# Copying finished attention contexts out of PSUM on VectorE instead of ScalarE

## The reference

```python
x = x + 0.5 * ffn(layernorm(x))
x = x + attention(layernorm(x))      # 16 heads of 16, causal, softmax, projection w_o and bias b_o
x = x + 0.5 * ffn(layernorm(x))      # the same FFN weights, which are +1 or -1

q, k, v = (h @ w.T split into 16 heads)
scores = q k^T / 4;  masked above the diagonal;  attn = softmax(scores)
ctx = attn @ v                        # (b, h, s, 16)
```

## Time and profile before

| | |
|---|---|
| median of 3 executions | 1556.35 us (1553.98 to 1558.93) |
| the profiled execution | 1555.03 us |
| its span, first to last instruction | 1553.3 us |
| granted clock of TensorE | 1.0 |
| busy: PE, DVE, ACT, POOL | 1533.4, 1118.7, 842.4, 194.9 us |
| chain that ended last | PE 97% |

### The profile page before, as it was taken

The page is one execution under the profiler, slowest core; times in us unless marked ns, Lnnn a source line. Parts: engine busy times, 40 slices in busy tenths (PEclk is TensorE's granted clock), DMA queues, the critical chain, the costliest instruction groups (busy, mean ns, idle before and its releaser), DMA issues.

```text
span 1553.3 us, 35454 instructions
## 1 busy us (share of the span) xinstructions
PE 1533.4 (99%) x14112; PEld 723.7 (47%) x14112; DVE 1118.7 (72%) x1618; ACT 842.4 (54%) x1706; POOL 194.9 (13%) x516
## 2 busy tenths in 40 slices
PE   7999999999999999999999999999999999999999
PEld 3555555555443333334333334333333555555554
DVE  6535543554669999999989998989896667666552
ACT  3223322332168888888888888888886222222221
POOL 4300000000011112121112212212220000000000
DMA  5122023502040222211222221222220222211210
GB/s 161 40 68 58 10 68 95 108 14 68 2 116 23 63 70 62 70 43 46 60 70 63 83 56 53 67 83 65 69 73 25 82 69 71 75 49 61 81 27 14
DMA packets 146275, 96.39 MB, mean 62 GB/s; under 512 B 106592, under 2 KB 125664, under 8 KB 146144
## 3 DMA queue, kind: packets, MB, share of 16 engines
q1 hardware_dynamic: 145712, 94.54, 21.3%
q10 hardware_dynamic: 432, 0.00, 0.0%
HBM read 49.15 MB, written 37.75 MB: 56 GB/s over the span
## 4 chain that ended last, share of the span: by engine, by line
PE 97%; ACT 1%; DVE 1%; SPq 1%; DMA 0%; issue 0%; DVEq 0%
PE ffn_mm L442 29%; PE ffn_mm L1338 18%; PE ffn_mm L1358 16%; PE ffn_mm L428 7%; PE ffn_acc L458 7%; PE ffn_acc L664 6%; PE ffn_tr L664 5%; PE ffn_mm L759 4%; PE ffn_acc L573 2%; PE ffn_acc L771 2%; PE ffn_tr L670 1%; PE ffn_tr L412 1%; ACT probs L1314 1%; PE ffn_acc L670 0%; DMA x_res<-L_attn_x 0%
## 5 line engine op out<-in xcount | busy, mean ns | idle before, releaser
L1314 ACT ACTIVATE probs<-ffn_mm 128x512 f32<-128x512 f32 (+1 forms) x960 | 471.0, 556 | 87.1 <-PE ffn_mm L1338 82.1
L685 DVE TENSOR_REDUCE m_part<-ffn_acc 128x2 f32<-128x1024 f32 (+1 forms) x348 | 370.1, 1063 | 33.0 <-PE ffn_acc L664 27.4
L1338 PE MATMUL ffn_mm<-qk 128*32 128x512 f16 (+7 forms) x5120 | 385.6, 353 | 4.2 <-ACT probs L1314 2.1
L442 PE MATMUL ffn_mm<-ffn_h1h,w 128*128 128x512 f16 x1024 | 388.3, 379 | 0.0
L442 PE MATMUL ffn_mm<-ffn_h1l,w 128*128 128x512 f16 x1024 | 388.1, 379 | 0.0
L685 DVE TENSOR_REDUCE m_part<-ffn_tr 128x2 f32<-128x1024 f32 (+2 forms) x292 | 308.6, 1057 | 37.6 <-PE ffn_tr L664 26.2
L508 ACT ACTIVATE ffn_h2h<-ffn_mm 128x512 f16<-128x512 f32 x128 | 76.4, 597 | 296.4 <-PE ffn_mm L442 295.0
L1358 PE MATMUL ffn_mm<-probs,v 128*32 128x512 f32 (+3 forms) x1920 | 236.0, 550 | 0.0
L1338 PEld LDWEIGHTS ffn_mm<-qk 66*32 66x32 f16 (+1 forms) x5120 | 134.9, 94 | 208.9 <-ACT probs L1314 91.0
L519 DVE SCALAR_TENSOR_TENSOR ffn_h2l<-ffn_mm,ffn_h2h 128x512 f16<-128x512 f32 x128 | 85.7, 687 | 167.1 <-ACT ffn_h2h L508 167.1
L442 PEld LDWEIGHTS ffn_mm<-ffn_h1h,w 128*128 128x128 f16 x1024 | 100.2, 98 | 118.9 <-issue 1.8
(11 more groups left out here) (134 smaller groups left out, 1212.5 us busy)
## 6 DMA issues: line engine op xcount, KB each, us to landing
qk<-qk_scr SPq DMA_DIRECT2D x256, 64.0 KB, 2.7
ctx_scr<-ctx_out SPq DMA_DIRECT2D x64, 256.0 KB, 2.5
qk<-ctx_scr SPq DMA_DIRECT2D x56, 256.0 KB
v_scr<-v_pad SPq DMA_DIRECT2D x32, 256.0 KB, 3.7
v<-v_scr SPq DMA_DIRECT2D x16, 512.0 KB, 4.0
x_res<-L_attn_x SPq DMA_DIRECT2D x8, 512.0 KB, 3.8
qk_scr<-qk_hi SPq DMA_DIRECT2D x32, 128.0 KB, 2.0
qk_scr<-qk_lo SPq DMA_DIRECT2D x32, 128.0 KB, 2.0
```

Of the source, the lines that this page charges most:

```text
L442: ins = nc.tensor.matmul(f.mm[:, m % 4, :], w1[:, kt, m * P:(m + 1) * P], part[:, kt, :], start=(kt == 0 and part is f.h1h), stop=(kt == H ...
L685: nc.vector.tensor_reduce(m_part[u][:, t, :, r], s_ps[slot][:, :, 0:w], AX.X, ALU.max).then_inc(sb.s_done, 1)
L1314: nc.scalar.activation(prob_tile(g, j, slice(c0, CH)), st_ps[bank(k)][:, c0:CH], ACT.Exp, scale=scale_now).then_inc(se.exp_done, 1)
L1338: ins = nc.tensor.matmul(st_ps[bank(k)][c:c + 32, c0:CH], k_part(pair % 2, h, rows, slice(kb * P + c, kb * P + c + 32)), q_part(pair % 2, ...
```

## The change

The copy of a finished context out of `ctx_ps` is made by VectorE (`tensor_copy`) instead of ScalarE (`activation` with Copy). `ctx_out` gets four parts, one for each chunk of a pair, each with a semaphore of its own. On VectorE the copy stands ahead of the items of its slot. The last two copies of the whole stage (chunks 2 and 3 of the last pair) are `late_context` in stage C: one behind `normalize_first`, one behind `dve_x`.

```diff
         self.ctx_st0 = new("ctx_st0")
         self.ctx_st1 = new("ctx_st1")
+        self.ctx_st2 = new("ctx_st2")
+        self.ctx_st3 = new("ctx_st3")
...
-            ctx_out = sbuf(st, "ctx_out", [P, 2, CH], F32)
+            ctx_out = sbuf(st, "ctx_out", [P, QCH, CH], F32)
...
-            ctx_st = (se.ctx_st0, se.ctx_st1)
+            ctx_st = (se.ctx_st0, se.ctx_st1, se.ctx_st2, se.ctx_st3)
+            late_ctx, late_stored = ctx_out, ctx_st
...
-                                 ctx_out[:, i % 2, :]).then_inc(ctx_st[i % 2], 16)
+                                 ctx_out[:, i, :]).then_inc(ctx_st[i], 16)
...
-                                            sp.wait_ge(sem, 8 * PAIRS * QCH)
+                                            sp.wait_ge(sem, 16 * PAIRS)
...
-                    sp.wait_ge(sem, 8 * BATCH * PAIRS * QCH)
+                    sp.wait_ge(sem, 16 * ALL_PAIRS)
...
             @block.vector
             def _(dve):
+                def evacuate(n):
+
+                    wait(dve, se.pv_done, ends[n] - PV_LAG + 1)
+                    if n == 0:
+                        dve.wait_ge(sa.qk_st, NCH * 128)
+                    wait(dve, ctx_st[n % QCH], n // QCH * 16)
+                    nc.vector.tensor_copy(ctx_out[:, n % QCH, :], ctx_ps[:, :]).then_inc(se.ctx_done, 1)
+
                 for pair in range(ALL_PAIRS):
                     for s in range(STEPS):
                         for j in range(4):
+                            if j == PV_POINTS[s] and pair * STEPS + s in ends[:-2]:
+                                evacuate(ends.index(pair * STEPS + s))
                             for _, owner, x, use in items(pair, s, j):
...
-                def evacuate(n):
-
-                    wait(act, se.pv_done, ends[n] - PV_LAG + 1)
-                    if n == 0:
-                        act.wait_ge(sa.qk_st, NCH * 128)
-                    wait(act, ctx_st[n % 2], n // 2 * 16)
-                    nc.scalar.activation(ctx_out[:, n % 2, :], ctx_ps[:, :], ACT.Copy).then_inc(se.ctx_done, 1)
...
-                        if j == PV_POINTS[s] and g in ends:
-                            evacuate(ends.index(g))
-                evacuate(len(ends) - 1)
...
+                def late_context(i):
+
+                    wait(dve, sb.pv_done, ends[i - QCH] - PV_LAG + 1)
+                    wait(dve, late_stored[i], (ALL_PAIRS - 1) * 16)
+                    nc.vector.tensor_copy(late_ctx[:, i, :], fa.mm[:, 3, :]).then_inc(sb.ctx_done, 1)
+
...
                 normalize_first()
+                late_context(QCH - 2)
                 dve.wait_ge(sb.bo_add, NCH * TPC)
                 add_attention(0)
                 dve_x_high(f, 0)
                 dve_x(f, 0)
+                late_context(QCH - 1)
                 dve_hidden(f, 0, range(HT), 0)
```

## The result

The kernel after takes 1590.34 us (median of 4 executions, 1589.8 to 1592.2). The kernel before, run beside it, took 1553.98, 1556.35, 1558.93 and once 3056.47 us; this last one is far outside the others, the ratio leaves it out, and the median of the other three is 1556.35. The ratio is 1.0217, 95% interval 1.0205 to 1.0229: the change makes the kernel 2.2% slower. The prediction said 1593, and a difference of 37.5 us. The medians differ by 34.0 us and the spans of the two profiled executions, 1553.3 and 1588.1, by 34.8.

What follows compares the result with a forecast made beforehand. TensorE was taken to wait for VectorE reduces behind which the copies queue. A 17.6, B 7.5, C 3.8 and D 8.6 make 37.5 us, so 1593.5; the likeliest case's own range is 1578 to 1602, overall 1564 to 1607.

Steps and rivals of the forecast that it cites:

- Place, not load: VectorE's load, 44.7 us in a 46.12 us pair, forbids nothing; each copy's place in its queue decides.
- A: Copy point s=4, j=0: VectorE waits 0.59 us for products, then copies for 0.61; TensorE loses 1.1 us a pair.
- B: Copy point s=8, j=3: the copy moves a reduce and the weight load after it by 0.61; taken as 0.5 us.
- C: Copy point s=14, j=1: the next chunk's first products wait for the copy, 0.2 to 0.25 late; taken as 0.25 us.
- D: Copy point s=2, j=2 of the next pair: the copy moves an item and its load by 0.61; taken as 0.57 us.
- A delay is passed on in full: Attention pairs: any delay of TensorE reaches the end unrecovered, as in pairs of 46.74 and 47.39 us.
- The second trial: The 47.39 us pair in the trace before, said to have grown by 1.27 us in the first trial's manner.
- Relief of ScalarE: Removing 64 copies frees 2.3 us a pair on ScalarE, valued near nothing: 0.1 us allowed at s=4, j=0.
- hide in VectorE's idle time: Rival: the copies fall in VectorE's 4.15 us of idle time a pair, so no change, 1556 us; chance 0.08.
- ScalarE's relief would win: Rival: exponentials set the pace, so freeing ScalarE gains about 22 us, giving 1534; chance 0.08.
- Partly absorbed: Rival: TensorE catches up between points or the s=4 wait is shorter; half the sum, 1575 us; chance 0.17.
- compounded: Rival: delays starve ScalarE and the mask step, whose waits add half as much again, 1612 us; chance 0.07.

Runs made afterwards that it cites:

- A alone: Against the kernel before: VectorE makes only the copy at s=4, j=0, ScalarE the other three; 47.25 us a pair, 1570.89 us, one execution.
- 16 columns on ScalarE: Kernel before, but from the second pair on ScalarE copies only 16 of the 512 columns of each context; 45.98 us a pair, ratio 0.9980.
- the load at idle places: Kernel before plus eight spare 256-element VectorE reduces a pair, ahead of items before which VectorE was idle; 46.11 us a pair, ratio 1.0019.
- B alone: Against the kernel before: VectorE makes only the copy at s=8, j=3, ScalarE the other three; 46.66 us a pair, 1562.41 us, one execution.
- the kernel with 46.72: Kernel after, but from the second pair on VectorE copies only 16 of 512 columns, waits kept; 46.72 us a pair, 1564.27 us, one execution.
- the five with 47.25 us or more: Kernel after (48.50), same with spare ScalarE copies (48.50), spare VectorE reduces at copy points (47.97), copies behind even items (47.48), VectorE copying only at s=4, j=0 (47.25).
- the load at the copy points: Kernel before plus four spare 512-element VectorE reduces a pair, ahead of the items next to the copy points; 47.97 us a pair, ratio 1.0175.

## Why the prediction was right, point by point

**Place, not load.** Right, and shown: 44.47 us of work at idle places costs a regular pair nothing, 43.99 at the critical ones costs 1.85.

**The point of each price.** A was put at 1.1 us and cost 1.02; B at 0.5, cost 0.54; C at 0.25, cost 0.22; D at 0.57, cost 0.60. The working held in most of its parts. The copy took 0.68 us and held the queue for 0.60 (715.10 to 715.70), taken as 0.69 and 0.61. By the table of the Trainium skill (VectorE: DVE Perf Modes, "The TRN2 errata — SBUF-src ops pay a fixed extra latency per instruction") the copy is an estimated 0.66, with VectorE slower than ScalarE. The trace agrees with the order (0.68 to 0.60) and is 3% above the size. The split of A into a wait and a copy holds: 0.53 for the wait and a copy of 16 columns, 0.51 for a copy's work without the wait. The working put VectorE's wait at A at 0.59 us; it measured 0.40 in the kernel after and 0.52 with A alone. At C the weight load of the products waited 0.28, and the products themselves start 0.15 later behind the scores ahead of them (729.81 after 729.43, against 715.68 after 715.45); this had been taken as 0.2 to 0.25.

**A delay is passed on in full.** Right within the regular pairs: the difference of starts stays between the points. B gave back 0.06 and C 0.12, which had been allowed for at B and not at C. The second trial that the prediction named, the pair of 47.39 us, wasn't quite of the same manner: TensorE stood still before a score matmul there, and its matmuls were busy 0.26 us longer (46.38 for 46.12). That nothing was regained holds for it too.

**Relief of ScalarE is worth next to nothing.** Right: 0.14 us a pair in the kernel before, where 0.1 had been allowed.

**Buffers and the last two copies are worth 0.** Right for the buffers (46.12 us a pair). The end costs nothing: from the copy at B of the last pair, on ScalarE in all three, to the end of the span it is 388.56 us in the kernel before, and 388.58 and 388.57 with only C or only D on VectorE, which have one of the two late copies each. In the kernel after the last but one copy waits 3.69 us for its products in time that VectorE had to spare.

**The sum.** 37.5 us were predicted, 34.8 came. The working adds 1.3 us to 1592.5 and writes 1593.5, where it is 1593.8; nothing hangs on it. The regular pairs make 15 x 2.38 = 35.7 us. From the last A to the end it is 0.8 us more (399.95 against 399.16), which is the A of the last pair, and the first copy comes 0.4 later: 36.9. What the sum left out is that the kernel before had irregular pairs, among them. All its pairs together lie 2.4 us above the regular length, and those of the kernel after 0.2 (the first takes 48.66, the others 48.49 to 48.53). The prediction read these rows as trials of how a delay travels and passed over what causes them. For the pair of 46.74 us the trace of before names it. The late item of the earlier trace rows stands on TensorE behind the first of these two; the second belongs to the pair of 47.39:

```profile
793.40 0.23 PE L664 MATMUL ffn_acc<-qk 64*128 64x128 f16 x2 [0.56 <-DMA qk<-qk_scr]
...
1030.84 0.40 PE L1338 MATMUL ffn_mm<-qk 66*32 66x256 f16 x7 [1.01 <-issue]
```

The first waits for q and k to land. Longer pairs leave the transfer more time, and the other kernels fit that: this same pair is too long by 1.1 us with 16 columns on ScalarE (45.98 a pair), 0.9 with four buffers only (46.12), 1.3 with the load at idle places (46.11), 0.4 and 0.6 with C and D alone (46.33, 46.63) and 0.1 with B alone (46.66), and regular in the kernel with 46.72 and in the five with 47.25 us or more. No experiment was made for it alone. The pair of 47.39 us is not of this kind: for its 1.01 us of waiting before a score matmul the profile names no releaser, and the pair is regular with A alone (47.25) and in the kernel after, but 1.3 us too long with the load at the copy points (47.97). Its cause stays open, and so does why it is gone in the kernel after; with it there, the difference would have been 1.3 us nearer to the 37.5.

**The rivals.** That the copies would hide in VectorE's idle time failed at the places where they stood, though the idle time is large enough, as the first load kernel shows. That ScalarE's relief would win failed by its size. "Partly absorbed" was right in kind, since VectorE does arrive later at A after a D, but by 0.12 us and not by half the sum. Nothing compounded: the single points add up to the whole.

No version tried here that copies all contexts beats the kernel before. Two thirds of ScalarE's copying time taken away brought 0.2%, and every copy on VectorE cost more than its share of that, at the places tried.

## What to carry to other kernels

Busy shares do not tell whether an engine can take over work. What tells is the instruction in front of which the new work would stand: if another engine's next step starts 0.1 us after that instruction ends, most of what is put before it is paid for (0.51 to 0.60 us for the 0.60 us of a copy or a spare reduce that had nothing to wait for, at A, B and D); if the engine is idle before it, the work cost a regular pair nothing here. And a copy that must wait for a producer should stand behind the work that is ready before it: moving it by one item gave back 0.6 of the 1.0 us at A.

## What the runs showed of the hardware

A copy of 16 fp32 columns out of PSUM takes 0.17 us on VectorE and 0.18 to 0.22 on ScalarE, one of 512 takes 0.68 and 0.60. So VectorE isn't the slower of the two for a small tile, and the 0.08 us by which it is slower for a large one lies in the columns. Less expected was that an engine with 1.6 us to spare in 46.11 (VectorE in the kernel with the load at idle places, 96% busy) can leave the time of a regular pair unchanged to 0.01 us.
